# The last local slot of the last layer in an order of its own: widening of the batch in front at its head, gates ahead of all exponentials, gated products in a buffer of their own

## What is computed

```python
for i in range(DEPTH):                      # DEPTH = 6
    x = attn_layer(shift_tokens(x), Wqkv[i], q_scale[i], k_scale[i], Wo[i]) + x
    x = ffn_layer(shift_tokens(x), ln_g[i], ln_b[i], W1[i], b1[i], W2[i], b2[i]) + x

def shift_tokens(t):                        # second half of the channels: one token later
    a, s = jnp.split(t, 2, -1)
    s = jnp.pad(s, ((0, 0), (1, 0), (0, 0)))[:, :-1]
    return jnp.concatenate([a, s], -1)

def ffn_layer(x, g, bln, W1, b1, W2, b2):
    mu = x.mean(-1, keepdims=True)
    var = ((x - mu) ** 2).mean(-1, keepdims=True)
    xn = (x - mu) / jnp.sqrt(var + 1e-05) * g + bln
    a, gate = jnp.split(xn @ W1 + b1, 2, -1)          # 2 x 682 columns
    return a * jax.nn.gelu(gate, approximate=False) @ W2 + b2
```

## Time and profile before

| | us |
|---|---|
| median of three runs | 2182.36 (2181.33 to 2184.53) |
| the profiled execution, its own time | 2184.0 |
| its span | 2182.2 |
| TensorE busy, of the span | 2094.1 (96%) |
| VectorE busy | 1678.5 (77%) |
| ScalarE busy | 1340.2 (61%) |
| GpSimd busy | 507.6 (23%) |
| mean granted TensorE clock | 0.988 |

### The profile page before, as it was taken

The page is one execution under the profiler, slowest core; times in us unless marked ns, Lnnn a source line. Parts: engine busy times, 40 slices in busy tenths (PEclk is TensorE's granted clock), DMA queues, the critical chain, the costliest instruction groups (busy, mean ns, idle before and its releaser), DMA issues.

```text
span 2182.2 us, 49532 instructions
## 1 busy us (share of the span) xinstructions
PE 2094.1 (96%) x16360; PEld 1702.3 (78%) x16360; DVE 1678.5 (77%) x4799; ACT 1340.2 (61%) x3916; POOL 507.6 (23%) x289
## 2 busy tenths in 40 slices
PE   5999999999998998999999999999999999999988
PEld 4777877777786676888888878887888888888877
DVE  6777677677665587888889888887889888988882
ACT  2667557556655245676667666766667666766652
POOL 2111111110111242232223222232223222322220
PEclk9999999999999999999999999999999999999999
DMA  3000000000000400021012011201120111111000
GB/s 118 7 11 1 6 12 1 6 12 1 6 26 0 155 11 13 14 71 32 27 38 70 14 33 52 71 14 33 52 71 13 34 51 45 31 33 52 14 13 20
DMA packets 46997, 70.00 MB, mean 32 GB/s; under 512 B 9093, under 2 KB 33717, under 8 KB 46517
## 3 DMA queue, kind: packets, MB, share of 16 engines
q1 hardware_dynamic: 44405, 62.21, 9.4%
q10 hardware_dynamic: 2368, 4.98, 0.6%
HBM read 50.54 MB, written 1.05 MB: 24 GB/s over the span
## 4 chain that ended last, share of the span: by engine, by line
PE 53%; DVE 4%; issue 3%; DMA 3%; ACT 2%; POOL 2%; SPq 0%; DVEq 0%; ACTq 0%; POOLq 0%
PE ps_loc L1553 17%; PE ps_loc L1659 9%; PE ps_loc L1630 6%; PE ps_loc L1669 4%; PE ps_loc L1603 4%; PE ps_loc L1592 4%; PE ps_loc L1619 4%; PE ps_loc L1572 3%; DMA late<-y_all 2%; POOL rnorm L2460 1%; PE ps_loc L1213 1%; ACT prob_loc L1882 1%; DVE norm L2082 1%; DVE w_low L2074 0%; PE ps_loc L1641 0%
## 5 line engine op out<-in xcount | busy, mean ns | idle before, releaser
L2460 POOL TENSOR_TENSOR rnorm<-norm_floor,half_loc 128x32 f32<-128x32 f32 x48 | 300.3, 6257 | 584.4 <-DVE norm_floor L2085 460.7
L1553 PE MATMUL ps_loc<-w_high,xT 128*128 128x512 f32 x1152 | 379.2, 410 | 0.7 <-ACT qk L1861 0.6
L1882 ACT ACTIVATE prob_loc<-prob_loc,top_loc 128x128 f32<-128x128 f32 x768 | 298.5, 397 | 44.3 <-DVE top_loc L2149 42.1
L1659 PE MATMUL ps_loc<-xnT_loc,w 128*128 128x256 f32 (+1 forms) x1056 | 252.0, 384 | 2.4 <-DVE kT_loc L2217 1.2
L673 ACT ACTIVATE prob<-prob,new_top 128x256 f32<-128x256 f32 x512 | 252.1, 497 | 0.0
L1553 PEld LDWEIGHTS ps_loc<-w_high,xT 128*128 128x128 f32 x1152 | 203.4, 188 | 50.4 <-issue 9.3
L2149 DVE CUSTOM_DVE_ANT_0 prob_loc<-ps_loc,const,rnorm 128x128 f32<-128x128 f32 x768 | 218.6, 344 | 27.2 <-PE ps_loc L1592 25.5
L1874 ACT ACTIVATE qT_loc<-ps_loc 128x512 f32<-128x512 f32 x96 | 57.3, 597 | 293.0 <-PE ps_loc L1572 293.0
L855 DVE CUSTOM_DVE_ANT_0 prob<-ps_cross,bias 128x256 f32<-128x256 f32 x512 | 185.0, 420 | 66.1 <-PE ps_cross L456 51.5
L1553 PE MATMUL ps_loc<-w_low,xT 128*128 128x512 f32 x576 | 227.3, 395 | 0.0
L1659 PEld LDWEIGHTS ps_loc<-xnT_loc,w 128*128 128x128 f32 (+1 forms) x1056 | 191.0, 190 | 28.5 <-DVE kT_loc L2217 2.4
(11 more groups left out here) (201 smaller groups left out, 4301.5 us busy)
## 6 DMA issues: line engine op xcount, KB each, us to landing
w_raw<-in_ffn_Wqkv_dram SPq DMA_DIRECT2D x24, 512.0 KB, 5.7
w_raw<-in_ffn_Wqkv_dram SPq DMA_DIRECT2D x24, 256.0 KB, 4.1
wo<-in_ffn_Wo_dram SPq DMA_DIRECT2D x24, 256.0 KB, 3.8
v_mid<-v_even SPq DMA_DIRECT2D x24, 256.0 KB, 3.3
v_mid<-v_odd SPq DMA_DIRECT2D x24, 256.0 KB, 3.5
w<-in_ffn_W_dram SPq DMA_DIRECT2D x12, 341.0 KB, 4.6
w<-in_ffn_W_dram SPq DMA_DIRECT2D x6, 640.0 KB, 5.1
ctx_raw<-in_ctx_dram SPq DMA_DIRECT2D x12, 256.0 KB, 2.7
```

Source lines behind the costliest of these rows:

```text
L1553: ins = pe.matmul(ps[:, DENSE + j % 2, :], xT[:, px, kk, t * P:(t + 1) * P], wqkv[pw][:, kk, col:col + 512], start=kk == 0 and n == 0, sto ...
L1659: ins = pe.matmul(ps[0:n, DENSE + m % 2, part * T:(part + 1) * T], w1[:, kk, col:col + n], xnT[:, kk, :], start=kk == 0, stop=kk == KD - 1)
L1882: ins = act.activation(pr, pr, ACT.Exp, bias=top[:, h, t:t + 1], scale=-1.0, accum_out=total[:, h, t:t + 1])
L2460: pool.tensor_tensor(rnorm[:, b % 2, t, :], norm2_floor[:, :], half[:, :], ALU.pow).then_inc(rnorm_done, 8)
```

## The change

The last layer's last slot gets lists of its own, `last_slot`, on TensorE, ScalarE and VectorE; the other slots keep theirs. Its order:

- TensorE: turn_qk, scores 0, turn_xn, scores 1, widen 0 and 1, scores 2, widen 2 and 3, scores 3, widen 4 and 5; then twice two turns of probabilities and an output piece, and so on to output 3; project_out; narrow.
- ScalarE: q_out, xn_out, all six gates, and only then the eight pairs of exponentials with the copies of turned probabilities and of outputs 0 and 3 between them.
- VectorE: moments of batch 2, ahead of k_out; k_out, normal, then minima 0 to 5 with the six gated products between them, then reciprocals and shares, with minima 6 and 7 where their buffers come free.
- The gated products go to `u_last`, which lies where w_high lies: free once the last projection is done. GpSimd waits for that and clears the last of its six parts (one 128 x 256 memset) before `norm` of batch 2, since narrow reads all 128 partitions of it and only 42 are written. `narrow` and `gated` take the buffer as an argument.

```diff
@@ place_layer_weights
+        with ExitStack() as shared:
+            self.u_last = self.sb("u_last", [P, FM, T], F32, shared)
         self.w_high = self.sb("w_high", [P, KD, 3 * INNER], F32R)
@@ TensorE
+            def last_slot(L):
+
+                a, f, fb = L + U * (B - 1), L + U * (B - 2), B - 2
+                turn_qk(a, False)
+                scores(a, 0)
+                turn_xn(f, False)
+                scores(a, 1)
+                widen(f, fb, 0, False)
+                widen(f, fb, 1, False)
+                scores(a, 2)
+                widen(f, fb, 2, False)
+                widen(f, fb, 3, False)
+                scores(a, 3)
+                widen(f, fb, 4, False)
+                widen(f, fb, 5, False)
+                turn_probs(a, 0)
+                turn_probs(a, 1)
+                out(a, L, B - 1, 0)
...
+                turn_probs(a, 6)
+                turn_probs(a, 7)
+                out(a, L, B - 1, 3)
+                project_out(a, B - 1)
+                narrow(f, fb, True, k.u_last)
@@ ScalarE
+            def last_slot(L):
+
+                a, f = L + U * (B - 1), L + U * (B - 2)
+                q_out(a)
+                xn_out(f, L, B - 2)
+                for m in range(FM):
+                    gates(f, m)
+                exps(a, 0)
+                exps(a, 1)
+                probs_out(a, 0)
+                exps(a, 2)
+                probs_out(a, 1)
+                exps(a, 3)
+                probs_out(a, 2)
+                o_out(a, 0)
+                exps(a, 4)
+                probs_out(a, 3)
+                exps(a, 5)
+                probs_out(a, 4)
+                exps(a, 6)
+                probs_out(a, 5)
+                exps(a, 7)
+                probs_out(a, 6)
+                probs_out(a, 7)
+                o_out(a, 3)
@@ VectorE
+            def last_slot(L, shifts):
+
+                a, f, fb = L + U * (B - 1), L + U * (B - 2), B - 2
+                moments(f, fb, shifts)
+                k_out(a)
+                normal(f, fb)
+                minima(a, B - 1, 0)
+                minima(a, B - 1, 1)
+                gated(f, 0, k.u_last)
+                minima(a, B - 1, 2)
+                gated(f, 1, k.u_last)
+                minima(a, B - 1, 3)
+                gated(f, 2, k.u_last)
+                minima(a, B - 1, 4)
+                gated(f, 3, k.u_last)
+                minima(a, B - 1, 5)
+                gated(f, 4, k.u_last)
+                gated(f, 5, k.u_last)
+                for pair in range(3):
+                    inverse(a, pair)
+                    share(a, pair)
+                minima(a, B - 1, 6)
...
+                add_attention(a, B - 1)
+                moments(a, B - 1, None, last=True)
+                add_ffn(f, fb)
@@ each engine's layer
-                slot(L, 3, True, not last, not last)
+                if last:
+                    last_slot(L)
+                else:
+                    slot(L, 3, True, True, True)
@@ GpSimd's layer
                 if not last:
                     tables(L + LAYER, i + 1)
+                else:
+                    pool.wait_ge(qkv_done, L + LAYER)
+                    pool.memset(k.u_last[:, FM - 1, :], 0.0)
                 norm(L + U * (B - 2), i, B - 2)
```

More of the change, by code:

```diff
@@ L1661, in widen, with narrow @@
                 ins.then_inc(f_full, 1 if m < FM - 1 else U - FM + 1)
-            def narrow(a, b, before_last=False):
+            def narrow(a, b, before_last=False, u=uT):
                 if b == 0:
@@ L1668, in narrow @@
                     for m in range(FM):
-                        ins = pe.matmul(ps[:, FFN_OUT, t * D:(t + 1) * D], uT[:, m, t * P:(t + 1) * P], w2[:, m, :],
+                        ins = pe.matmul(ps[:, FFN_OUT, t * D:(t + 1) * D], u[:, m, t * P:(t + 1) * P], w2[:, m, :],
                                         start=m == 0, stop=m == FM - 1)
@@ L1755, in slot @@
                 if ffn:
-                    narrow(f, fb, not ahead)
+                    narrow(f, fb)
+            def last_slot(L):
[15 more added lines that the diff above has]
+                out(a, L, B - 1, 0)
+                turn_probs(a, 2)
+                turn_probs(a, 3)
+                out(a, L, B - 1, 1)
+                turn_probs(a, 4)
+                turn_probs(a, 5)
+                out(a, L, B - 1, 2)
+                turn_probs(a, 6)
[3 more added lines that the diff above has]
+                narrow(f, fb, True, k.u_last)
             def layer(L, first, last):
@@ L2003, in layer @@
                 slot(L, 2, True, True, not last, split=not last)
-                slot(L, 3, True, not last, not last, late=not last)
+                if last:
+                    last_slot(L)
+                else:
+                    slot(L, 3, True, True, True, late=True)
             lin_xn_out, lin_queries_out, yn_out = linear_scalar(act)
@@ L2210, in normal, with gated @@
                 ins.then_inc(xn_done, U)
-            def gated(a, m):
+            def gated(a, m, u=uT):
                 n = FWIDE[m]
@@ L2216, in gated @@
                 dve.wait_ge(gate_done, a + after(m, FM - 1))
-                dve.scalar_tensor_tensor(out=uT[0:n, m, :], in0=ps[0:n, DENSE + m % 2, 0:T],
+                dve.scalar_tensor_tensor(out=u[0:n, m, :], in0=ps[0:n, DENSE + m % 2, 0:T],
                                          scalar=vec[0:n, V_B1A + m:V_B1A + m + 1], in1=gate[0:n, m % 2, :],
@@ L2341, in slot @@
                     add_ffn(f, fb)
+            def last_slot(L, shifts):
[19 more added lines that the diff above has]
+                minima(a, B - 1, 6)
+                inverse(a, 3)
+                share(a, 3)
+                minima(a, B - 1, 7)
+                inverse(a, 4)
+                share(a, 4)
+                o_out(a, 1)
+                for pair in range(5, PAIRS):
+                    inverse(a, pair)
+                    share(a, pair)
+                o_out(a, 2)
+                add_attention(a, B - 1)
+                moments(a, B - 1, None, last=True)
+                add_ffn(f, fb)
             def layer(L, i, shifts, last_shifts, first, last):
@@ L2346, in layer @@
                 slot(L, 2, i, shifts, True, True, not last, split=not last)
-                slot(L, 3, i, shifts, True, not last, not last, late=not last)
+                if last:
+                    last_slot(L, shifts)
+                else:
+                    slot(L, 3, i, shifts, True, True, True, late=True)
             moments_x(3)
```

## The result

The change makes the kernel slower: 2203.75 us (median of four runs, 2200.93 to 2209.57) against 2181.85 us before, a ratio of 1.0098 with an interval of 1.0084 to 1.0113. That is 21 us. The forecast was 2198.5, 16 us, with a range up to 2202.5: the right side and the right places, but too little, and outside the range.

What follows compares the result with a forecast made beforehand. TensorE was taken as the bound in the steady part, with waits in the last slot. Stall at the head and lost order +8.1 and half clock in the tail +8.0 made +16.1 on 2182.36: 2198.5 us, range 2189 to 2202.5.

Steps and rivals of the forecast that it cites:

- The head: Start of the last slot: VectorE waits for the late transfer until 2112.9, TensorE idles 6.9 us, widening starts at 2121.9.
- the first term of the sum: In the last slot: stall at the head and lost order make project_out 8.1 us later.
- case B: Rival: in the serial tail the clock holds at full, so only +8.1, 2190.5 us; chance 0.22.
- The serial tail at half clock: Behind the last gate: table load 1.28 us, four rounds of 5.6 us, project_out at 2160.9, 16.1 us late.
- I leave both out of the sum and in the range: Half clock in project_out, up to 1.7 us more, and in the last batch's widening, either way: not summed.
- 8 pairs of exponentials at 1.16 (2120.75 to 2121.91): ScalarE's exponentials in the serial tail: 1.16 us a pair, 9.3 us of its 14.1 us of work.
- Stall at the head and lost order +8.1, half clock in the tail +8.0: The last slot's delay split into two terms, 16.1 us together.
- C: Rival: transfer landed by 2106.9, no stall at the head, full-clock tail, project_out 0.6 early, 2181.8 us; chance 0.07.
- E: Rival: half clock also in part of the widening and project_out, +20, 2202.5 us; chance 0.10.
- A: The forecast itself: stall at the head and half-clock tail, 2198.5 us, own range 2194 to 2202; chance 0.58.
- D: Rival: gaps filled, TensorE bound throughout, 8.4 us gained, 2174.0 us; chance 0.03.
- The range: For the whole kernel's time: 2189 to 2202.5 us.

Runs made afterwards that it cites:

- again: The changed kernel run unedited on another chip, against the kernel before: ratio 1.0095, 2206.93 us beside 2183.99.
- e4: The kernel before with VectorE's moments of batch 2 moved ahead of k_out in the last slot: ratio 1.0039 to the kernel before.
- e1: The changed kernel with the 127-row shift issued as two transfers, 112 and 15 rows: ratio 1.0075 to the kernel before.
- e2: The changed kernel with k_out put back ahead of moments on VectorE: ratio 1.0097 to the kernel before.
- e12: The changed kernel with four unused transposes in each of the tail's last four gaps only: ratio 1.0086 to the kernel before.
- e8: The kernel before with another last-slot order, moments behind six pairs of minima, widenings between later turns: ratio 0.9988 to the kernel before.
- e15: The changed kernel with shortened last-slot exponentials, two of 256 columns per pair instead of four of 128: ratio 1.0086 to the kernel before.
- e5: The changed kernel with unused transposes keeping TensorE busy between the steps of the tail: ratio 1.0074 to the kernel before.
- e16: The changed kernel with the edits of e1 and e5 and the shortened exponentials of e15: ratio 1.0036 to the kernel before.
- e7: The changed kernel with the edits of e1 and e5 together: ratio 1.0039 to the kernel before.

## Where the forecast was right, and which steps of its sum failed

Taken from the start of project_out in slot 2, forecast and first profile after stand so:

| point | forecast | measured |
|---|---|---|
| widening starts | 28.1 | 28.0 |
| last gate ends | 40.4 | 40.9 |
| first turn of probabilities | 44.0 | 45.0 |
| project_out starts | 67.1 | 68.2 (again: 68.7) |
| end, from there | 37.5 | 39.1 (again: 40.9) |

**The head** was right in each step: landing, 7 us of idle in turn_qk, half clock behind it, widening at full clock with VectorE and ScalarE covered. e4 priced it at 8.4 us alone. That the first term of the sum is also near this, 8.1, is chance: it is the price of case B, the stall and a tail at full clock together.

**The serial tail at half clock** was right in place and kind. ScalarE's table load of 1.28 us stands where it was forecast, and the rounds too:

```profile
2132.76 1.28 ACT L1917 ACT_TABLE_LOAD   x1
2134.05 0.40 ACT L1917 ACTIVATE prob_loc<-prob_loc,top_loc 128x128 f32<-128x128 f32 x1
...
2135.61 0.39 ACT L1917 ACTIVATE prob_loc<-prob_loc,top_loc 128x128 f32<-128x128 f32 x1
```

```profile
2136.83 1.12 PE L1605 MATMUL ps_loc<-const,prob_loc 128*128 128x128 f32 x4 [4.68 <-DVE prob_loc L2229]
...
2142.63 1.12 PE L1605 MATMUL ps_loc<-const,prob_loc 128*128 128x128 f32 x4
...
2148.91 1.12 PE L1605 MATMUL ps_loc<-const,prob_loc 128*128 128x128 f32 x4
...
2154.71 1.11 PE L1605 MATMUL ps_loc<-const,prob_loc 128*128 128x128 f32 x4
...
2160.05 7.14 PE L1632 MATMUL ps_loc<-wo,qT_loc 128*128 128x256 f32 x32 [0.85 <-ACT qT_loc L1931]
```

The turns of pairs 0, 2, 4 and 6 start 5.8, 6.3 and 5.8 us apart, against 5.6. In the first profile the clock rose in the last round and made up for this, so the 23.2 us from the first turn to project_out, against 23.1 forecast, are in part luck. In e1 and e2, where half clock lasts to the end of the tail, they are 24.5. Of the Trainium skill's 2.7 us for a table load with its drain ("ScalarE: Activation LUTs", "What ACT_TABLE_LOAD costs") the trace shows the load alone, 1.28 us: the first exponential starts at 2134.05, as it ends.

**What failed in the sum.** Three steps. The first is the one that put the time beyond the range: "I leave both out of the sum and in the range", half clock in project_out and in the last widening. It was not nothing. The last widening took 1.5 us more in both profiles, project_out 1.8 more in the second. The 1.8 is half clock that the tail leaves behind, and it belongs in the sum. The 1.5 is not from the tail (e12) and came without the change too (e8). With 1.1 to 1.6 for the slot this makes 18.8 and 21.1 us in slot and end, the second being what the ratios of both groups give.

Second, a term: "8 pairs of exponentials at 1.16 (2120.75 to 2121.91)". These two rows are three instructions apart, and a pair is four: 1.55 us, as from 2134.05 to 2135.61 above. The term is 12.4 us, not 9.3. At half clock this hardly counts, as e15 shows; 0.4 us of it is in the 1.0 us by which the first turn is late.

Third, the split "Stall at the head and lost order +8.1, half clock in the tail +8.0". With the tail at full clock and the stall in place (e5) the slot is 14.7 us longer than before, where B had 8.1; and from there to the changed kernel it is only 2.6 to 3.1 us, where the sum had 8.0 (4 to 5 without the cost of e5's transposes, by my estimate). The total for the slot came out near because it was summed directly from rounds at half clock, and the two terms erred in opposite directions. What B and C had wrong is the full-clock tail: 18.7 us from the table load to project_out (2134.2 to 2152.9), with ScalarE's pieces laid end to end. e5 has 24.3. The mis-sized exponentials are the smaller part of these 5.6 us: e16, whose pairs take 1.0 us, less than the 1.16 of the sum, still has 22.7. Some 1.5 us are e5's own transposes, and the rest, some 2.5, is by this reckoning the waiting of both engines for each other, which the sum for full clock left out. Case C, which e7 comes nearest to, fails for the same reason: it has 8.3 us where C had -0.6.

**The rivals.** E, "half clock also in part of the widening and project_out: +20, 2202.5", came nearest, 2203.75 against 2202.5; it had a chance of 0.10 and was the mechanism of A with the term that A had left out. It came true in the last widening in both profiles and in project_out in the second only; the widening of the slot itself ran at full clock. B was wrong about the clock: it fell in the empty 4.6 us. C was excluded by the landing (8.60 us), and by e1 and e7, in which the transfer lands early, it would not have been even with the kernel before. D fails in every run.

**The range** ended at the value of E, with nothing above it, although two terms had been left open on the same side.

## What to carry to other kernels

Ahead of moving a step to the head of a queue, look up when its latest input lands, not when the step used to start: here 6 us of other work hid a transfer that ran on one DMA engine. A block with nothing beside it is priced by the waits of its engines for each other, at full clock too, and then by the clock that it leaves behind, also in the work right after it. And when a duration is taken from the distance of two rows, count the instructions between them.

## What the runs showed that I had not expected

- The kernel before itself spent 13.6 us at half clock in slot and end of its profile, and 78 transposes of no use, 56 in the slot's gaps and 22 in the epilogue, bought 0.29% (0.14 to 0.43).
- Removing a stall at the head of a slot (6.1 us) gave back only 4 to 5 us in the runs, since the half clock moved to other work; with the clock held, the same edit was worth 8 by the ratio (e5 to e7, 1.0074 to 1.0039) and 5.7 by slot and end. The intervals of these differences are some 4 us to either side.
- One transfer of 127 rows takes 8.6 us behind the issue that follows it, 112 rows and 15 rows 2.3 and 2.1 behind their own.
